# Wide scatter tables four columns at a time, zero transfers on GpSimd's queue, count tiles summed on VectorE

## What is computed

```python
out = x @ root + bias
for r in range(weight.shape[0]):
    mask = (edge_type == r).astype(x.dtype)
    sums = jax.ops.segment_sum(msgs * mask[:, None], dst, num_segments=n)
    cnt = jax.ops.segment_sum(mask, dst, num_segments=n)
    mean = sums / jnp.maximum(cnt, 1.0)[:, None]
    out = out + mean @ weight[r]
```

## Time and profile before

| | us |
|---|---|
| median of 3 runs | 1830.52 |
| lowest, highest | 1827.37, 1830.97 |
| the profiled execution | 1828.82 |
| its span | 1827.3 |
| PE busy | 1738.4 |
| DVE busy | 989.4 |
| ACT busy | 461.8 |
| POOL busy | 712.6 |

### The profile page before, as it was taken

One profiled execution on the slowest core, in us unless ns is written; L12 is line 12 of the kernel. 1 busy time (PEld: TensorE's weight loads), 2 busy tenths in 40 slices (PEclk: granted clock), 3 DMA queues, 4 the chain that ended last, 5 costly groups with the idle time before them and its releaser, 6 DMA issues.

```text
span 1827.3 us, 27442 instructions
## 1 busy us (share of the span) xinstructions
PE 1738.4 (95%) x9548; PEld 1438.4 (79%) x9548; DVE 989.4 (54%) x2498; ACT 461.8 (25%) x888; POOL 712.6 (39%) x613
## 2 busy tenths in 40 slices
PE   6998999999999999999999999846999999999999
PEld 4775699978777777878787877634999888879987
DVE  6997999972625454452526386877613234352311
ACT  3327788930101011010101154433000000111100
POOL 3100010036363544536453544000785551446862
PEclk9999999999999999999999999858999999999999
DMA  4435333243131212122233532110454350113322
GB/s 132 142 115 163 124 109 94 94 129 94 47 97 38 87 40 80 52 68 69 63 89 122 168 113 86 28 48 7 131 183 142 103 155 25 47 47 126 91 72 67
DMA packets 132122, 168.42 MB, mean 92 GB/s; under 512 B 14383, under 2 KB 75963, under 8 KB 131767
## 3 DMA queue, kind: packets, MB, share of 16 engines
q1 hardware_dynamic: 104213, 128.21, 23.6%
q10 hardware_dynamic: 21730, 22.51, 3.8%
q0 software_dynamic: 6080, 16.40, 2.9%
HBM read 135.51 MB, written 25.30 MB: 88 GB/s over the span
## 4 chain that ended last, share of the span: by engine, by line
PE 81%; DVE 10%; DMA 3%; ACT 2%; DVEq 2%; issue 2%; POOL 1%; SPq 1%; ACTq 0%
PE ps L363 21%; PE ps L364 21%; PE ps L365 21%; PE ps L1406 9%; DMA w_stage<-in_stream 2%; PE ps L1001 1%; DVE w_lo L314 1%; PE ps L1371 1%; PE ps L923 1%; DVE key_start L869 1%; POOL w_lo L272 1%; PE ps L1326 1%; SPq L1051 1%; DMA nat<-in_x 1%; DVE scan L784 1%
## 5 line engine op out<-in xcount | busy, mean ns | idle before, releaser
L363 PE MATMUL ps<-w_hi,xt_hi 128*125 128x512 f32 x1320 | 539.4, 409 | 12.1 <-DVE xt_lo L552 3.5
L252 POOL TENSOR_TENSOR w_hi<-w_stage,zero 128x512 fp32r<-128x512 f32 x258 | 278.1, 1078 | 680.0 <-PE ps L365 650.8
L364 PE MATMUL ps<-w_lo,xt_hi 128*125 128x512 f32 x1320 | 523.6, 397 | 0.0
L365 PE MATMUL ps<-w_hi,xt_lo 128*125 128x512 f32 x1320 | 522.0, 395 | 0.0
L255 POOL TENSOR_TENSOR w_lo<-w_stage,w_hi 128x512 fp32r<-128x512 f32 x258 | 351.2, 1361 | 20.2
L363 PEld LDWEIGHTS ps<-w_hi,xt_hi 128*125 128x125 f32 x1320 | 247.0, 187 | 70.9 <-DVE xt_lo L552 4.3
L365 PEld LDWEIGHTS ps<-w_hi,xt_lo 128*125 128x125 f32 x1320 | 246.4, 187 | 63.3
L364 PEld LDWEIGHTS ps<-w_lo,xt_hi 128*125 128x125 f32 x1320 | 246.6, 187 | 53.4
L363 PE MATMUL ps<-xt_hi,w_hi 128*128 128x314 f32 x736 | 240.9, 327 | 0.8 <-DVE ring L2612 0.7
L365 PE MATMUL ps<-xt_hi,w_lo 128*128 128x314 f32 x736 | 226.0, 307 | 0.0
L364 PE MATMUL ps<-xt_lo,w_hi 128*128 128x314 f32 x736 | 225.8, 307 | 0.0
(11 more groups left out here) (433 smaller groups left out, 2178.5 us busy)
## 6 DMA issues: line engine op xcount, KB each, us to landing
w_stage<-in_stream SPq DMA_DIRECT2D x374, 256.0 KB, 2.7
pre<-ring POOLq DMA_DIRECT2D x30, 250.0 KB, 5.6
adj<-zeros SPq DMA_DIRECT2D x19, 321.8 KB
a_qt<-pre_t SPq DMA_DIRECT2D x18, 312.5 KB, 3.8
a_qt<-pre_t ACTq DMA_DIRECT2D x14, 312.5 KB
pre_t<-ring_t POOLq DMA_DIRECT2D x12, 312.5 KB, 3.1
pre_t<-ring_t ACTq DMA_DIRECT2D x12, 312.5 KB
a_vx<-pre SPq DMA_DIRECT2D x9, 312.5 KB
```

Source lines behind the costliest of these rows:

```text
L252: POOL.tensor_tensor(w_hi[:, q, :], w_stage[:, q % NST, :], zero[:].to_broadcast([128, 512]), ALU.add).then_inc(S("hi_done"), 1)
L363: PE.matmul(dst, l_hi, r_hi, start=first, stop=False)
L364: PE.matmul(dst, l_hi, r_lo, start=False, stop=False)
L365: return PE.matmul(dst, l_lo, r_hi, start=False, stop=last)
```

## The change

Three things.

*The scatter.* Four columns, a *quad*, are handled by one pair of DVE instructions: `sc_hi` becomes 240 x 4 and `sc_lo` 128 x 4, the columns innermost, made by comparing `iota_by4` (now 240 x 4) with four values per edge row that are repeated. There are 42 quads and 3 sets of tables. ACT makes the codes of three quads in four, one column at a time, reading and writing in steps of four; DVE makes those of each fourth quad (n % 4 == 3) in one instruction, behind the tables of the next quad. PE's scatter matmul reads both operands in steps of four, 8 bytes. Quad n has its place behind slot 9n/5 of the stage. In each step, ACT's split and DVE's split both come behind the step's first quad. ACT evacuates group 3 behind quad 4, DVE group 4 behind the first quad of step 9.

*The zero transfers.* The first 8 are issued by GpSimd, before it stores group 3, with a semaphore of their own; SP keeps 11.

*The relation loop.* For relations after the first DVE adds the 5 tiles of counts (`counts_sum`), splits the sum in two float16 parts, and PE needs 4 matmuls (`sums_pe`) in place of 10. The relay `ag_scaled` goes: ACT waits for DVE's scaling itself.

```diff
+    def gpsimd_program(mk_zeros, mk_ranked, zero_counts):
+        for g in range(G_PRE0):
+            if g == 3:
+                wait(POOL, mk_zeros)
+                wait(POOL, mk_ranked)
+                for i in range(EARLY):
+                    zero_counts(POOL, i, "ld_zero")
             for m in range(T):
...
+    sc_hi = [at(f"sc_hi{i}", [P, NCHUNK, 4], BF16, r_hot + i * 1920) for i in range(3)]
+    sc_lo = [at(f"sc_lo{i}", [P, 128, 4], BF16, r_hot + 5760 + i * 1024) for i in range(3)]
+    sc_code = [at(f"sc_code{i}", [P, 128, 4], BF16, r_hot + 8832 + i * 1024) for i in range(3)]
...
+    def by_dve(n):
+        return n % 4 == 3
...
+    def scatter_dve(n):
+        DVE.wait_ge(S("sc_pe"), 4 * n + 4)
+        DVE.tensor_tensor(sc_hi[n % 3][:], iota_by4[0:P],
+                          e_hi16[:, 4 * n:4 * n + 4].unsqueeze(1).to_broadcast([P, NCHUNK, 4]), ALU.is_equal)
+        DVE.tensor_tensor(sc_lo[n % 3][:], iota_by4[0:P, 0:128],
+                          e_lo16[:, 4 * n:4 * n + 4].unsqueeze(1).to_broadcast([P, 128, 4]), ALU.is_equal).then_inc(S("sc_hot"), 1)
+        if n and by_dve(n - 1):
+            code = DVE.tensor_tensor(sc_code[(n - 1) % 3][:], sc_lo[(n - 1) % 3][:],
+                                     e_code16[:, 4 * n - 4:4 * n].bitcast(BF16).unsqueeze(1).to_broadcast([P, 128, 4]), ALU.mult)
+            code.wait_op(S("sc_hot"), low_made(n - 1), "sem-ge")
+            code.then_inc(S("sc_hot"), 1)
+
+    def scatter_act(n):
+        if by_dve(n):
+            return
+        ALE.wait_ge(S("sc_hot"), low_made(n))
+        for c in columns(n):
+            ALE.activation(sc_code[n % 3][:, :, c % 4], sc_lo[n % 3][:, :, c % 4], ACT.Copy,
+                           scale=e_code[:, bass.ds(c, 1)].bitcast(F32)).then_inc(S("sc_scaled"), 1)
+
+    def scatter_pe(n):
+        for c in columns(n):
+            if by_dve(n):
+                PE.wait_ge(S("sc_hot"), code_made(n))
+            else:
+                PE.wait_ge(S("sc_scaled"), scaled(c))
+            PE.matmul(slot_ps, sc_code[n % 3][:, :, c % 4], sc_hi[n % 3][:, :, c % 4], start=False, stop=False).then_inc(S("sc_pe"), 1)
...
+        def place(n):
+            return n * 9 // 5
+
+        def quads(s):
+            return [n for n in range(QUADS) if place(n) // T == s]
...
+        for s in range(SC_GROUPS * KT):
+            for n in quads(s):
+                scatter_act(n)
+                if n == quads(s)[0]:
                     split_act(chunk_beside(s))
+                if n == 4:
+                    evacuate_plain(SC0 - 1)
+                    load_bias(SC0)
+            if not quads(s):
+                split_act(chunk_beside(s))
...
+        for s in range(SC_GROUPS * KT):
+            for n in quads(s):
+                scatter_dve(n)
+                if n == quads(s)[0]:
                     split_dve(chunk_beside(s))
-            if s == KT:
-                evacuate(SC0)
+                if s == KT + 1 and n == quads(s)[0]:
+                    evacuate(SC0)
+            if not quads(s):
+                split_dve(chunk_beside(s))
...
+    def counts_sum(r):
+
+        t_ = adj[:, bass.ds(r * T * NB, T * NB)].rearrange("p (t x) -> p t x", x=NB)
+        DVE.tensor_tensor(tile_pairs[:], t_[:, 0:2], t_[:, 2:4], ALU.add)
+        DVE.drain()
+        DVE.tensor_tensor(tile_sum[:], tile_pairs[:, 0], tile_pairs[:, 1], ALU.add)
+        DVE.drain()
+        DVE.tensor_tensor(tile_sum[:], tile_sum[:], t_[:, 4], ALU.add)
+        DVE.drain()
+        DVE.tensor_copy(sum_hi[:], tile_sum[:])
+        DVE.drain()
+        DVE.tensor_tensor(sum_lo[:], tile_sum[:], sum_hi[:], ALU.subtract).then_inc(S("a_ready"), 1)
...
+    def sums_pe(r):
+
+        PE.wait_ge(S("a_ready"), 2 * r + 1)
+        for i in range(2):
+            bank, h0, hn = ag_bank(i)
             PE.wait_ge(S("ag_free"), r * 18 + i + 1)
+            dst = ps[:, bank, 0:hn]
+            PE.matmul(dst, ones16[0:P, :], sum_hi[:, h0:h0 + hn], start=True, stop=False)
+            PE.matmul(dst, ones16[0:P, :], sum_lo[:, h0:h0 + hn], start=False, stop=True).then_inc(S("ag_full"), 1)
...
-            ALE.wait_ge(S("ag_scaled"), r * 16 + j + 1)
+            ALE.wait_ge(S("ag_free"), r * 18 + j + 6)
...
-
-            DVE.wait_ge(S("ag_free"), 3 + r * 18 + i + 1)
-            DVE.sem_inc(S("ag_scaled"), 1)
...
             counts_split(r + 1)
-            DVE.wait_ge(S("a_ready"), r + 2)
+            counts_sum(r + 1)
+            DVE.wait_ge(S("a_ready"), 2 * r + 3)
```

More of the change, by code:

```diff
@@ L735, in bucket_counts @@
         DVE.memset(e_field[:, EC:EW], 0)
+        DVE.memset(e_code16[:, EC:], 0)
+        DVE.memset(e_lo16[:, EC:], -1.0)
+        DVE.memset(e_hi16[:, EC:], -1.0)
         DVE.tensor_scalar(e_tile[:], ed_src[:], float(P), None, ALU.is_ge)
@@ L822, in rank_fields @@
         DVE.drain()
+        DVE.tensor_copy(e_code16[:, 0:EC], e_code[:, 0:EC])
+        DVE.drain()
         DVE.tensor_scalar(e_code[:, 0:EC], e_code[:, 0:EC], 16, None, ALU.logical_shift_left)
@@ L888, in positions @@
         DVE.drain()
-        DVE.tensor_copy(e_hi[:, 0:EC], e_tmpi[:])
+        DVE.tensor_copy(e_hi16[:, 0:EC], e_tmpi[:])
         DVE.drain()
@@ L892, in positions @@
         DVE.drain()
-        DVE.tensor_copy(e_lo[:, 0:EC], e_tmpi[:])
+        DVE.tensor_copy(e_lo16[:, 0:EC], e_tmpi[:])
     def packed_buckets(mk):
@@ L907, in packed_buckets @@
         return sig(DVE.drain(), "dve_step")
[L910 to L919, removed]
@@ L921, in scatter_pe, with columns, low_made, code_made @@
-    def scatter_pe(c, j):
-        PE.wait_ge(S("sc_scaled"), c + 1)
-        PE.matmul(slot_ps, sc_code[j][:], sc_hi[j][:], start=False, stop=False).then_inc(S("sc_pe"), 1)
+    def columns(n):
+        return range(4 * n, min(4 * n + 4, EC))
+    def by_dve(n):
+        return n % 4 == 3
+    def low_made(n):
+        return n + 1 + max(n - 1, 0) // 4
+    def code_made(n):
+        return n + 2 + n // 4 + 1
+    def scaled(c):
+        return c + 1 - 4 * ((c // 4 + 1) // 4)
+    def scatter_dve(n):
[9 more added lines that the diff above has]
+            code.then_inc(S("sc_hot"), 1)
@@ L944, in hist_row @@
             DVE.wait_ge(S("hi_pe"), c - 4 * (NROWS - 1))
-        DVE.tensor_tensor(hot_row[c // 4 % NROWS][:], iota_by4[:],
+        DVE.tensor_tensor(hot_row[c // 4 % NROWS][:], iota_by4[:, 0:128],
                           slot_row[:, c:c + 4].unsqueeze(1).to_broadcast([128, 128, 4]),
@@ L1021, in beside @@
             "g (b f) -> f (g b)", f=128), allow_slow_non_contiguous=True).then_inc(S("ld_bt"), 16)
+        mk_zeros = sig(ALE.activation(zeros[:], zero[0:P, :].to_broadcast([P, ZERO_RUN]), ACT.Copy), "act_step")
         for g in range(3):
@@ L1043, in beside, with zero_counts @@
         LAST_AHEAD = C_HAND + 4 + NST - 1
[L1044 to L1053, removed]
+        def place(n):
+            return n * 9 // 5
+        def quads(s):
+            return [n for n in range(QUADS) if place(n) // T == s]
+        def zero_counts(eng, i, landed):
+            eng.dma_start(adj[:].bitcast(F32)[:, i * ZERO_RUN:(i + 1) * ZERO_RUN], zeros[:]).then_inc(S(landed), 16)
+        gpsimd_program(mk_zeros, mk_ranked, zero_counts)
         for c in range(SC0 * KT, (SC0 + SC_GROUPS) * KT):
@@ L1076, in between @@
                     PE.matmul(slot_ps, zero16[:, 0:128], zero16[:], start=True, stop=False)
-                if 0 <= s < SC_STEPS:
-                    for c, j in columns(s):
-                        if j * T // sc_per == m:
-                            scatter_pe(c, j)
-                            if c == EC - 1:
-                                PE.matmul(slot_ps, zero16[:, 0:128], zero16[:], start=False,
-                                          stop=True).then_inc(S("sc_pe"), 1)
+                for n in quads(s):
+                    if place(n) % T == m:
+                        scatter_pe(n)
+                        if n == QUADS - 1:
+                            PE.matmul(slot_ps, zero16[:, 0:128], zero16[:], start=False,
+                                      stop=True).then_inc(S("sc_pe"), 1)
             return between
@@ L1307, in counts_split @@
                           ALU.subtract).then_inc(S("a_ready"), 1)
+    tile_pairs = at("tile_pairs", [P, 2, NB], I16, R_EXTRA)
+    tile_sum = at("tile_sum", [P, NB], I16, R_EXTRA + 2560)
+    sum_hi = at("sum_hi", [P, NB], F16, R_EXTRA)
+    sum_lo = at("sum_lo", [P, NB], F16, R_EXTRA + 1280)
+    def counts_sum(r):
[7 more added lines that the diff above has]
+        DVE.tensor_copy(sum_hi[:], tile_sum[:])
+        DVE.drain()
+        DVE.tensor_tensor(sum_lo[:], tile_sum[:], sum_hi[:], ALU.subtract).then_inc(S("a_ready"), 1)
     counts_split(0)
```

107 lines of the change are left out of this document (46 added, 61 removed).

## The result

The changed kernel takes 1832.78 us (median of 20 runs, 1830.92 to 1835.16), the kernel before 1830.00 in the same comparison: ratio 1.0015, 95% interval 1.0009 to 1.0021. The time lies 2.8 us above it, inside the range and inside 0.2%, but on the other side of no change: a small loss was measured where a small gain was forecast. The profiled span grew from 1827.3 to 1830.9, +3.6 us.

What follows compares the result with a forecast made beforehand. PE, ACT and DVE were taken as nearly level in the scatter, ACT and DVE 0.15 us a round above PE. Terms +11.3 - 5.5 - 5.7 - 0.7 = -0.6 us led to 1830.0 us, range 1820 to 1839.

Steps and rivals of the forecast that it cites:

- the price of the strided moving operand: PE's scatter matmul reading in steps of four: taken as 0.10 us a column, bounds 0.10 or two times that.
- PE's step: In the scatter, 15 matmuls of 512 columns and 11 scatter matmuls: 4.73 us when PE is catching up.
- +11.3: Scatter stage: sum in us of the later start, rounds and evacuations, before what the transfers give back.
- the ties: Scatter: ACT's and DVE's splits wait on each other; ACT idles 1.73 or 2.64 us, rounds 5.04 to 5.95 against 4.88.
- The double price: Scatter: moving operand at 0.20 us a column; the stage ends 2.9 us later, the whole takes 1833 us.
- The rival in which PE bounds the scatter: Scatter: ACT or DVE work ahead, the ties don't bind; stage -9 us, whole 1815 us; chance 14%.
- ACT on strided tables: Scatter codes on ACT: 0.35 us a code taken, bound 0.45; 0.40 makes the stage 5.5 us longer, 0.45 makes it 11.
- the second rival: Scatter: strided table slows ACT (1835.5 or 1841 us), or moving operand at double price (1833); together 20%, at 1836 us.
- The transfers: Eight zero transfers moved from SP's to GpSimd's queue: ACT's split no longer waits for chunk 40, -5.5 us.
- the hole's cold stretch: Scatter: PE idles almost wholly 160 to 166 us, then clock 0.50 for six microseconds; taken as equal to a new one.
- The counts: Relation loop: 4 matmuls for 10 in seven relations, -5.7 us; DVE's 2.9 us covered by its 5.84 us idle.
- The relay: Relation loop: `ag_scaled` removed, shortening five handovers of 0.15 in the first relation: -0.7 us, between 0 and -1.5.

Runs made afterwards that it cites:

- The old scatter without its hole: Kernel before with its 11-column scatter, the eight zero transfers on GpSimd's queue and no relay: ratio 0.9964, scatter 87.7 us for 93.2.

## Why the prediction was wrong

The step that failed is the price of the strided moving operand. The forecast took 0.10 us a column, with 0.20 as the other bound, and let the tied rounds hide what might lie between; so it left PE off the path of the scatter. The price is 0.22, which lifts PE's step to 5.9 us, above most rounds, and puts PE on the chain; with the operand read consecutively the ratio falls from 1.0015 to 0.9979. By the Trainium skill's page "SBUF — State Buffer", section "Door 1: The DMA port swizzle", a step of four bf16, with two hits in a 16-byte line, should have run at full rate. The runs contradict it for this operand: full rate with four hits in a line (step of two), half with two. The forecast had no row of a strided moving operand; it chose the bound that changed nothing, though at 0.20 us a column PE's own step, 4.73 + 11 x 0.10 = 5.8 us, was already above most of its rounds.

Point by point:

- *The stage.* Forecast: group 5 ends at 234.7. It ended at 239.5. The old scatter without its hole takes 87.7 us from the first table; of the +11.3, 0.8 was a later first table (it came 0.2 later), so the ties were to add 10.5. With a consecutive operand they add 95.5 - 87.7 = 7.8. The stride adds the other 7.9. So the tie term was 2.7 too large and the stride 7.9 too small. The double price had been worked out as +2.9 in the stage and 1833 in the whole. The whole measured 1832.8, but that is in part luck: by that sum the profiled execution was to lose 2.3 us, and its span lost 3.6; the kernel before had a median 0.5 us lower in the comparison than on record, and the too large ties made up for part of the stride.
- *The ties* are there as described: idle of 1.66 and 2.57 us for 1.73 and 2.64, each DVE split waiting for ACT's. The rounds are shorter because a code takes 0.30 us for 0.35; with the consecutive operand the first round is 4.77 us where 5.04 was forecast. Two things differ in the codes from before: ACT waits once for four of them and not before each, and it reads and writes in steps of four. The runs don't part the two.
- *PE's step* was forecast at 4.73 to 5.2 us, under the ties. At 5.9 it is above most of them. The rival in which PE bounds the scatter came true on its other side: as a loss.
- *ACT on strided tables*: no slowing, 0.30 us a code. That part of the second rival falls; its other part, the moving operand at double price, is what came.
- *The transfers*: no split waits for `w_stage`, as forecast. Counted from the old scatter, as in the forecast's sum, the move is worth its 5.5 us; beside the new one it is worth nothing measurable, since slower rounds remove the same wait. The sum is right, but the credit depends on the order in which the parts are counted.
- *The granted clock* fell to 0.92 in 138 to 150 us, behind PE's idle there, and the hole's cold stretch went. The forecast had set the two equal. By the traces the old one had cost nothing and the new one costs about 1.2 us, since PE is the bound behind it.
- *The counts*: -5.5 for -5.7. But DVE's part of them takes 6.6 us, not 2.9: the add of 1252 elements takes 1.65 us where 0.8 was taken, two adds of 626 elements take 1.43 and 1.07 us where 0.48 each were taken, the cast 1.26 for 0.32; why they are that slow was not looked into. The cover of 5.84 us was used whole. It cost nothing that the trace shows: no engine's wait ends with the maximum.
- *The relay*: -1.1 for -0.7, in the first relation only, as forecast.

## What to carry to other kernels

Before a table's layout is turned to suit its maker, price how its reader walks it: here PE's moving operand of bf16 was read at full pace in steps of 4 bytes and at half pace in steps of 8, so these columns could be interleaved in pairs, not in fours. When a table's price is known only between two bounds, work out each engine's step at the dearer one and see whether the path changes. Where two limits lie within a few tenths of a microsecond, neither edit alone shows its worth; test them together before one is given up. Moving a transfer off a blocked queue paid here only while its consumer was early enough to wait for it.

## What the runs showed of the hardware

The moving operand (125 x 240 bf16) took 0.11 us a column consecutive or in steps of two elements, 0.22 in steps of four. At a granted clock of 0.50 four columns in steps of four took 0.72 us to the next matmul (0.68 at 1.00), two consecutive ones 0.29 (0.14 at 1.00). The weight load of 128 columns in steps of four took 121 ns (100 before), while one of 125 columns takes 193 ns. DVE's comparison of 16-bit elements four columns at a time took 654 ns for 960 and 419 for 512; two columns at a time 403 for 480. Its int16 adds of 626 elements took 1.07 to 1.43 us, its cast of 626 from int16 to float16 1.26.
